# Eight expert slots behind the last gate, their order from the counts of 15 groups, and results written to (token, choice) rows

## The reference

```
conv   = grouped conv1d(x over the channels, 9 taps, 4 groups) + cond @ c_weight.T + bias
logits = conv @ W_gate + b_gate                    # 8 experts
i1, i2 = top_k(logits, 2)
x      = x + mean_k relu(conv @ W_e[i_k] + b_e[i_k])
att    = softmax(MLP(cond))                        # 8 weights per sample
x      = x + (sum_k att_k W_k applied to x over the channels + bias) @ dequant(qweight) + bias
```

## Time and profile before

| | us |
|---|---|
| median of 3 runs | 546.04 |
| lowest, highest | 544.32, 546.64 |
| the profiled execution, its time | 544.99 |
| the profiled execution, its span | 543.2 |
| PE busy | 513.6 |
| DVE busy | 339.4 |
| POOL busy | 147.0 |
| ACT busy | 121.7 |

### The profile page before, as it was taken

One profiled execution on the slowest core, in us unless ns is written; L12 is line 12 of the kernel. 1 busy time (PEld: TensorE's weight loads), 2 busy tenths in 40 slices (PEclk: granted clock), 3 DMA queues, 4 the chain that ended last, 5 costly groups with the idle time before them and its releaser, 6 DMA issues. The chain is left out here.

```text
span 543.2 us, 10445 instructions
## 1 busy us (share of the span) xinstructions
PE 513.6 (95%) x2486; PEld 344.6 (63%) x2487; DVE 339.4 (62%) x1003; ACT 121.7 (22%) x277; POOL 147.0 (27%) x162
## 2 busy tenths in 40 slices
PE   6969999999978999999999999999979899999996
PEld 5859999999955344444444444444427677777774
DVE  3466888888873563333333333333762899999996
ACT  2122223234310111111111111111121222222221
POOL 8042444544463000000000000000004766556520
PEclk9999999999988999999999999999998999999999
DMA  4999778877444844444444444444465899888862
GB/s 116 379 319 330 254 242 298 289 272 239 170 154 149 213 155 151 155 155 155 155 155 154 153 151 154 151 151 157 128 218 174 266 312 294 291 276 288 299 199 97
DMA packets 84823, 114.32 MB, mean 210 GB/s; under 512 B 15197, under 2 KB 51853, under 8 KB 83509
## 3 DMA queue, kind: packets, MB, share of 16 engines
q1 hardware_dynamic: 57936, 56.49, 32.5%
q0 software_dynamic: 10528, 33.75, 18.8%
q10 hardware_dynamic: 16328, 23.72, 12.5%
HBM read 67.48 MB, written 46.45 MB: 210 GB/s over the span
## 5 line engine op out<-in xcount | busy, mean ns | idle before, releaser
L989 PE MATMUL bank<-we,hT 128*128 x536 | 230.9, 593 | 4.0 <-DVE hT L815 4.0
L989 PEld LDWEIGHTS bank<-we,hT 128*128 128x128 f32 x536 | 101.5, 190 | 132.3 <-issue 132.1
L454 POOL DMA_INDIRECT we<-result_d,gidx x64 | 68.4, 1069 | 284.9 <-issue 276.9
L824 DVE TENSOR_TENSOR ring_a<-bank,be_bc 128x512 f32<-128x512 f32 x71 | 48.9, 689 | 126.4 <-PE bank L989 117.9
L957 PE MATMUL bank<-wconv,phases 128*128 128x128 f32 x768 | 93.0, 279 | 4.9 <-ACT phases L478 4.9
L957 PEld LDWEIGHTS bank<-wconv,phases 128*128 128x128 f32 x768 | 90.2, 195 | 5.3 <-ACT phases L478 5.3
L532 ACT ACTIVATE ring_b<-ring_a 128x512 f32<-128x512 f32 x71 | 44.7, 630 | 208.2 <-DVE ring_a L824 201.6
L435 POOL DMA_INDIRECT lists_d<-htok,row_i x64 | 62.9, 983 | 87.6 <-issue 63.4
L815 DVE STREAM_TRANSPOSE hT<-htok 128x512 f32<-128x512 f32 x71 | 49.8, 701 | 9.0 <-DMA htok<-lists_d 9.0
L1029 PE MATMUL bank<-mix_bd,we 128*128 128x128 f32 x256 | 36.6, 286 | 2.3 <-DVE we L858 2.3
L945 PE MATMUL bank<-wg,hT 128*128 128x136 f32 x256 | 37.4, 289 | 1.1 <-ACT htok L488 1.1
(11 more groups left out here) (164 smaller groups left out, 406.4 us busy)
## 6 DMA issues: line engine op xcount, KB each, us to landing
htok<-lists_d SPq DMA_DIRECT2D x284, 64.0 KB, 2.4
result_d<-ring_b ACTq DMA_DIRECT2D x71, 256.0 KB, 2.4
xt<-in_x SPq DMA_DIRECT2D x64, 256.0 KB, 4.3
we<-in_L_ffn_W_e SPq DMA_DIRECT2D x8, 1024.0 KB, 6.5
out<-orow SPq DMA_DIRECT2D x32, 256.0 KB, 3.9
lists_d<-orow SPq DMA_DIRECT2D x8, 256.0 KB, 7.5
be_bc<-in_L_ffn_b_e ACTq DMA_DIRECT2D x1, 2048.0 KB, 11.2
rows_r<-ctx_d SPq DMA_DIRECT2D x1, 1920.0 KB, 10.7
```

What stands on the lines that cost most here:

```text
L454: pool.indirect_dma_start(found[:, j, k, :], None, result_d, bass.IndirectOffsetOnAxis(ap=gidx[:, j, k:k + 1], axis=0), bounds_check=NT * ...
L824: dve.tensor_tensor(ring_a[:, j % 2, :], ps_exp[j % 2][:, :], be_bc[:, bass.ds(expert, 1), :].rearrange("p a n -> p (a n)"), ALU.add).then ...
L989: mm = pe.matmul(ps_exp[j % 2][:, :], hT[:, j % 2, p * P:(p + 1) * P], we[:, bass.ds(expert, 1), p, :].rearrange("m a n -> m (a n)"), star ...
```

## The change

It has four parts.

1. **Early slots.** `base` after 15 groups is turned into a first table, `tab_early`, by 19 small DVE operations spread over groups 16 to 26 (`early_table`). It names 8 slots, all of them full blocks of 128 rows that those 15 groups have already filled. SP loads the first four behind the scatters of the 15 groups. PE runs slot 0 directly behind the last gate, and the rank counts, the mixing kernels and the table's transpose between slots. The 34 idle transposes are gone. The final table counts the taken blocks out, and its slots follow from slot 8 on; the number of products stays the same.
2. **(token, choice) rows.** Each row of a list gets two more numbers (`LK` = 514): 2 x token, and the first choice's expert. A row is now 2,056 bytes. ACT writes them (L532 of the new kernel), SP loads them with a fifth DMA per slot (`keys`, 8 bytes a row), and DVE makes the pair's row from them (`pair_i`). A pad row has a key beyond the bound and is skipped.
3. **Result stores.** POOL scatters a slot's results by one indirect DMA to `pairs_d`, in place of ACT's direct store. Stage 3 loads the two results of a group by one direct DMA of 512 KB from SP, in place of POOL's two gathers; `find_places` and the index copies on ACT are gone.
4. **Order and buffers.** Lists load into `xt`, four slots ahead, and DVE transposes two slots ahead into four buffers (`lT`, of which `hT` is two). Side work moves: mixing bias to slot 6, masks and dequantizing to slots 9 to 13, the rank rows to 17 to 19. Loops over groups are looped up to group 16 instead of 24.

The core of the diff:

```diff
+            for s in range(NT):
+                pool.wait_ge(result_ready, s + 1)
+                pool.wait_ge(pair_ready, s + 1)
...
+                pool.indirect_dma_start(pairs_d, bass.IndirectOffsetOnAxis(ap=pair_i[:, s % DR:s % DR + 1], axis=0),
+                                        ring_b[:, s % U, :], None, bounds_check=2 * N * C - 1,
+                                        oob_is_err=False).then_inc(result_out[s % U], 16)
...
-            sp.wait_ge(head_out, 16 * E)
-            for s in scattered:
-                sp.wait_ge(s, 32 * (NG // U))
-            sp.wait_ge(tab_ready, 2)
+            sp.wait_ge(early, N_EARLY)
+            for j, s in enumerate(scattered):
+                sp.wait_ge(s, 32 * len(range(j, counted, U)))
...
+                    if isinstance(a, int) and a == EARLY:
+                        sp.wait_ge(head_out, 16 * E)
+                        for i, scat in enumerate(scattered):
+                            sp.wait_ge(scat, 32 * len(range(i, NG, U)))
+                        sp.wait_ge(tab_ready, 2)
...
+                    sp.dma_start(keys[:, ja, :], lists_d[bass.ds(row, P), L:LK]).then_inc(list_in[ja], 16)
...
+            def load_pairs(a):
+                sp.dma_start(found[:, a % FR, :, :], pairs_g[a]).then_inc(pairs_in[a % FR], 16)
+
+            for i, s in enumerate(result_out):
+                sp.wait_ge(s, 16 * len(range(i, NT, U)))
+            for g in range(U):
+                load_pairs(g)
...
+            def transpose_list(a, ja):
+
+                wait(dve, list_in[ja], (a - ja) * (80 // XR) + 80)
+                wait(dve, exp_done, a - AHEAD + 1)
+                dve.transpose(lT[:, ja, :].rearrange("m (p h r) -> m h p r", p=PH, h=MH),
+                              xt[:, ja, :].rearrange("r (h p l) -> r h p l", h=MH, p=PH)).then_inc(lT_ready, 1)
+                wait(dve, result_out[ja], 16 * ((a - DR - ja) // U + 1))
+                dve.scalar_tensor_tensor(pair_i[:, a % DR:a % DR + 1], keys[:, ja, 1:2], slot_expert[:, a:a + 1],
+                                         keys[:, ja, 0:1], ALU.not_equal, ALU.add).then_inc(pair_ready, 1)
...
+            for g in range(hi1, NG - 2):
+                step1_late(g, g % U)
+            early_wait()
+            transpose_list(0, 0)
+            step1(NG - 2, (NG - 2) % U)
+            transpose_list(1, 1)
+            step1(NG - 1, (NG - 1) % U)
+            dve.wait_ge(tok_done, NG - 1)
+            transpose_list(2, 2)
+            step1(NG, NG % U)
+            dve.wait_ge(tok_done, NG)
+            transpose_list(3, 3)
+            dve.wait_ge(be_in, 16)
+            add_bias(0, 0)
+            step1(NG + 1, (NG + 1) % U)
+            add_bias(1, 1)
...
-            for _ in range(WARM):
-                pe.transpose(bank[6][:, 0:P], ident[:, :], ident[:, :])
...
+            gate_and_rows(NG - 1, (NG - 1) % U)
+            pe.wait_ge(early, N_EARLY)
+            pe.wait_ge(we_in, 16 * E)
+            product(0, 0)
+            count_ranks(NG - 2, (NG - 2) % U)
+            product(1, 1)
+            count_ranks(NG - 1, (NG - 1) % U)
+            mix_layers(NG + 1 - mlp_first)
+            for s in range(2, 5):
+                product(s, s % U)
+            pe.wait_ge(tab_ready, 1)
+            pe.transpose(ps_misc[0:3, 256:256 + P], tab_f[:, :], ident[:, :]).then_inc(tab_done, 1)
+            pe.matmul(ps_misc[:, 256 + P:256 + 2 * P], tab_f[:, 1:2].to_broadcast((P, P)), ident[:, :], start=True, stop=True).then_inc(tab_done, 1)
+            for s in range(5, EARLY):
+                product(s, s % U)
+            pe.wait_ge(tab_ready, 2)
+            stepped(pe, step2, lo2, 16, hi2, NT)
```

More of the change, by code:

```diff
@@ L32 @@
 XR = 4
+FR = 8
+DR = 8
+LK = L + 2
+NO_PAIR = 1 << 20
+EARLY = 8
+AHEAD = 4
 RS = B + 2
@@ L265, in build_program @@
         table = sem("table")
+        early = sem("early")
         tab_done = sem("tab_done")
@@ new lines, in load_x @@
+            def load_x(a):
+                sp.dma_start(htok[:, a % XR, :], x_g[a]).then_inc(x3_in[a % XR], 16)
+            for s in range(-U, lo2):
+                list_step(s, s % U)
+            for g in range(XR):
+                load_x(g)
+            stepped(sp, list_step, lo2, lo2, hi2 - U, NT - U)
+            def load_pairs(a):
+                sp.dma_start(found[:, a % FR, :, :], pairs_g[a]).then_inc(pairs_in[a % FR], 16)
+            for i, s in enumerate(result_out):
+                sp.wait_ge(s, 16 * len(range(i, NT, U)))
@@ L479, in step1 @@
                              ps_ph[:, :].rearrange("k (h s l) -> k h s l", h=MH, s=SUB)).then_inc(ph_ready, 1)
+                b = g - 2
+                if live(b, NG):
+                    jb = (j - 2) % U
+                    wait(act, expert_ready, b + 1)
+                    act.copy(token_list[:, jb, L:LK],
+                             expert_of[:, bass.ds(b, 1), 0:2].rearrange("p a k -> p (a k)")).then_inc(key_ready, 1)
                 a = g - 1
@@ L544, in _, with store_mix @@
-            for s in range(SUB):
-                rows = slice(s * C, (s + 1) * C)
-                act.dma_start(mix_bd[rows, :, rows],
-                              mix_d.rearrange("(g s) i o -> s i g o", s=SUB)[s]).then_inc(mix_in, 16)
-            stepped(act, step2, 1, lo2, hi2, NT)
+            def store_mix():
+                act.wait_ge(mlp_ev, 11)
+                act.wait_ge(mixb_split, 3)
+                act.dma_start(mixb_d[0], mixb_hi[:, :].bitcast(F32)).then_inc(mix_out, 16)
+                act.dma_start(mixb_d[1], mixb_lo[:, :].bitcast(F32)).then_inc(mix_out, 16)
+                act.dma_start(mix_d, mix_sb[:, :, :]).then_inc(mix_out, 16)
@@ new lines, in load_mix @@
+            def load_mix():
+                act.wait_ge(mixbd_zero, 1)
+                act.wait_ge(mix_out, 48)
+                act.wait_ge(mixb_one, 1)
+                for half in range(2):
+                    pair = 2 * B + 2 * half
+                    act.dma_start(token_rows[pair:pair + 2, :].bitcast(F32),
+                                  mixb_d[half:half + 1].rearrange("a n c -> a (n c)").to_broadcast((2, N * C))).then_inc(mix_in, 16)
+                for s in range(SUB):
+                    rows = slice(s * C, (s + 1) * C)
+                    act.dma_start(mix_bd[rows, :, rows],
+                                  mix_d.rearrange("(g s) i o -> s i g o", s=SUB)[s]).then_inc(mix_in, 16)
@@ L550, in step3 @@
+            for s in range(lo2):
+                step2(s, s % U)
+                if s == 6:
+                    store_mix()
+            for s in range(lo2, 12):
+                step2(s, s % U)
+                if s == 8:
+                    load_mix()
+            stepped(act, step2, 12, 12, hi2, NT)
             def step3(g, j):
@@ new lines, in add_bias @@
+            def add_bias(s, j):
+                if isinstance(s, int) and s < EARLY:
+                    expert = dve.value_load(tab_early[0:1, 1, s:s + 1], min_val=0, max_val=E - 1)
+                else:
+                    expert = dve.value_load(tab[1:2, bass.ds(s - EARLY, 1)], min_val=0, max_val=E - 1)
+                wait(dve, exp_done, s + 1)
+                wait(dve, result_ready, s - 1)
+                dve.tensor_tensor(ring_a[:, j % 2, :], ps_exp[j % 2][:, :],
+                                  be_bc[:, bass.ds(expert, 1), :].rearrange("p a n -> p (a n)"), ALU.add).then_inc(sum_ready, 1)
@@ L790, in find_places @@
-            def find_places(first, last):
-                rows2 = row_of[:, :, :].rearrange("p g k -> p (g k)")
-                expert2 = expert_of[:, :, :].rearrange("p g k -> p (g k)")
-                for e in range(first, last):
-                    if e == 0:
-                        then(dve.tensor_scalar(shift_s[:, :], expert2, 0.0, offs[:, 0:1], ALU.is_equal, ALU.mult))
-                    else:
-                        then(dve.tensor_scalar(shift_e[:, :], expert2, float(e), offs[:, e:e + 1], ALU.is_equal, ALU.mult))
-                        then(dve.tensor_tensor(shift_s[:, :], shift_s[:, :], shift_e[:, :], ALU.add))
-                if last == E:
-                    dve.tensor_tensor(place_i[:, :, :].rearrange("p g k -> p (g k)"), rows2, shift_s[:, :], ALU.subtract).then_inc(place_ready, 1)
```

310 lines of the change are left out of this document (178 added, 132 removed).

## The result

The changed kernel takes **538.56 us**, median of 4 runs (536.77 to 540.77); the kernel before, measured beside it, takes 545.96 (4 runs, 544.32 to 546.64). The ratio is 0.9868, with a 95% interval of [0.9838, 0.9897]: faster by 7.4 us. Forecast were 530.0 and a range of 526 to 538. The direction was right, the gain less than half of the 15.6 us that the sum gave, and the time lies just above the range. A second set of runs, beside its own runs of the kernel before, gives 0.9857 (experiment 9).

A forecast was written before the change was run, and what follows sets the result against it. PE was taken to bound all three stages. Takeover -13.2, handover -1.0 and start of stage 3 -1.4 sum to -15.6, from the profiled 544.99 to 529.4; half of 1.05 put back gives 530.0 us, range 526 to 538.

The forecast's parts named there:

- Does one wait?: Check of the takeover into stage 2: no early product waits, and product 8 has a slack of 4 to 5 us.
- Stage 2, 0: Steady expert slots: no change in time, queue work fits each 3.43 us slot, fifth load covered by four slots of lead.
- bound of -9: Smallest gain allowed for the takeover into stage 2, if one product waits a full slot's time; the other bound was -15.
- the -13.2 forecast: Takeover from last gate into stage 2: 16.1 us of gap and stalls can go, 2.9 stay on PE.
- Handover, -1.0: From last product to stage 3's first mixing: about 1.0 us gained through sooner idle matmuls and direct loads, range -3 to +4.
- The second rival: Longer handover to stage 3: 512 KB loads land after 8.6 us, not 3.4, giving 535 us; chance 8%.
- The rule of the Trainium skill that I weighed: Handover: issue DMAs under DVE's work from ACT or SP, not GpSimd; by it the sum would be 2.8 us higher.
- Start of stage 3, -1.4: From first to third mixing in stage 3: 6.52 us becomes 5.1 with groups 0 to 3 loaded in one go.
- Stage 1, 0 (to +2): Stage 1: added table operations and longer scatter rows cost PE nothing, range 0 to +2 us.
- The takeover stalls: Rival at the start of stage 2: a list, table or bias is late once, giving 535 us; chance 10%.
- The 72% for 530: Whole kernel: the chance given to the time coming out as forecast, 530.0 us.
- the signs named ahead: Traces of being right: product 0 within 0.5 us of last gate, clock 1.00, mixing kernels 1.8 us, last product near 390.5.

The follow-up runs named there:

- experiment 9: The changed kernel, unaltered, run and profiled a second time: 537.53 us, ratio 0.9857.
- experiment 3: Changed kernel with stage 3's x loads issued behind the last list and the mixing load behind slot 24, not 8: 531.71 us, ratio 0.9748.
- experiment 7: experiment 3 with both last rank counts and the mixing kernels put back ahead of product 0: 538.41 us, ratio 0.9866.
- experiment 5: experiment 3 without each list's fifth load (keys), result rows made from slot number and lane: 531.72 us, ratio 0.9739.
- experiment 10: experiment 3 with the quantized words' eight loads spread over groups 16 to 23 and the biases' load at 24, not group 3: 527.38 us, ratio 0.9639.
- experiment 12: experiment 3 with only the 2 MB load of the biases moved, to group 24: 529.14 us, ratio 0.9614.
- experiment 8: The kernel before, unchanged, profiled a second time: 542.78 us, one run.
- experiment 11: The kernel before with the words' eight loads at groups 24 to 31 and the biases' load at 31, not group 3: 547.99 us, ratio 0.9956.
- experiment 1: Changed kernel with only the four x loads for stage 3 moved, behind the last list: 533.05 us, ratio 0.9769.
- experiment 2: Changed kernel with only the mixing load moved, from behind slot 8 to behind slot 24: 532.94 us, ratio 0.9755.
- experiment 6: experiment 5 with list rows of 2,048 bytes again, not 2,056: 531.59 us, ratio 0.9744.

## Why the prediction was right or wrong

**Where it failed: "Does one wait?" and "Stage 2, 0", both terms that the x loads and the mixing load should have been in.** I followed product by product up to slot 8, found slacks of 4 to 5 us, and stopped where the table was in use. For the rest I wrote "four slots of lead are 13.7 us" and took the queues' work per slot, 1.6 us of 3.43 on SP, as if each slot had the same. The diff puts four loads of 256 KB into SP's queue between lists 11 and 12 and the mixing load behind slot 8 on ACT. Neither has a term in my sum, though the 1.36 us in the earlier trace rows stand right behind such a load at its old place. Measured, the two together cost 7.3 us, 4.94 of waiting and most of the rest low clock (6.1 in the second profile). My bound of -9 for the term allowed one late product and no fall of the clock; the profile showed -5.3.

**The term's mechanism and size were right where nothing meets.** In experiment 3, gate end to last product end is 234.7 us against 247.3, so -12.6 against the -13.2 forecast. The idle time of the kernel before, its low clock and its waits in the first slots did go, and experiment 7 shows that the order of counts and products carries 6.7 us of it.

**Handover, -1.0.** In experiment 3: 15.09 us against 16.12, so -1.0. In the changed kernel +0.1: the idle matmuls took 12.69 us and not 11.25, and ended at 417.5, after the data. This isn't a cost of the stall: the changed kernel's second profile has the stall, 11.27 us of idle matmuls and 15.10 us of handover, and experiments 5, 10 and 12 have no stall and 15.8 to 15.9. The three profiles of the kernel before and its variant have 15.84 to 16.21. So the -1.0 was met in about half of the profiles; the sum took the length of the idle matmuls as fixed, and it changes with the clock by 1 us and more. The data path had the forecast's length: the last result scatter is issued at 408.74, 7.6 us after the last product's end (forecast 7.0), the first pairs' load at 410.94, and DVE's first addition starts at 414.80:

```profile
414.80 0.69 DVE L987 TENSOR_TENSOR we<-token_list,we 128x512 f32<-128x512 f32 x1 [8.60 <-DMA we<-pairs_d]
```

That is T + 13.65; my steps put it at 10.3 + 3.4 = 13.7. The second rival, loads that land after 8.6 us, didn't come: DVE starts 3.86 us after the issue begins, and the median of all 32 is 4.7.

**POOL as issuer beside DVE.** The page's group says what the result scatters cost:

```profile
L506 POOL DMA_INDIRECT pairs_d<-ring_b,pair_i x71 | 70.5, 992 | 164.7 <-DVE pair_i L867 112.1
```

71 issues at a mean of 992 ns, against 980 in the earlier trace rows, so POOL's issues weren't longer beside DVE's work. The rule of the Trainium skill that I weighed, in "SBUF — State Buffer", section "Summary: rules for kernel authors", speaks of DVE in its 2x and 4x perf modes alone. I had taken it for all of DVE's work, and no run here shows whether an operation of DVE was in such a mode.

**Start of stage 3, -1.4:** -1.9, a little small; 4.58 to 4.71 us in all eleven profiles with the change, 6.52 to 6.70 in three without it. **Stage 1, 0 (to +2):** PE's pace is unchanged, but its beginning is not; two traces against nine give about +2 at convolution 7, from a cause that stays open (experiments 8 to 12). I had looked at 60 to 80 us alone, where the stage is steady.

**The rivals.** "The takeover stalls", 10% at 535, was what happened, with the price too small: it took one product's time and no clock loss. It was named for a list, the table or a bias within the sequence that I had followed, not for the loads that came behind it. The 72% for 530 was too much for a sequence that I had followed through 8 slots of 71. Of the signs named ahead, product 0's distance, the mixing kernels and the steady convolutions came out as written; the full clock throughout and the absence of idle time did not, and the last product ended at 401.2 where 390.5 was named. The sign of being wrong, idle time ahead of products 5 to 8, didn't show either: the wait came at product 12.

## What to carry to other kernels

When a change removes a gap, list every DMA that it puts into the stretch behind it, on all queues, with bytes and packet size, and follow the loads until the lead is full again, not only until the handover is done. Two loads that are each harmless there may not be together; move one of them to where the lead is full (here 6 to 7 us for a few moved lines). And count a PE wait of some microseconds dearer than its length: here 4.94 and 3.49 us in stage 2 were followed by about 2.1 and 1.7 us lost to the low clock, though not every wait of that length was (below).

## What the runs showed of the hardware that was not expected

- Four loads of 128 KB in pieces of about 142 bytes occupied ACT for 7.33 us beside the x loads, for 4.05 us in experiment 1 without them, and for 3.77 us in experiment 3. ACT's next operation, the relu at 202.72, stood idle 7.69 us behind it.
- With the engines' share at 1.26, a list of four 64 KB loads and the keys was there 7.4 us after its last issue and 9.7 after its first; in experiment 2, without the mixing load, 2.8 and 4.9 us after them.
- Behind PE's idle time of 4.94, 3.49 and 2.44 us the granted clock fell to 0.50. In the kernel before once more, 3.47 us of idle time ahead of convolution 5 left it at 1.00, and so did 3.7 us ahead of experiment 6's idle matmuls. In experiment 10 it fell to 0.56 at 162 to 166 us, where PE had been busy since 152.46 behind idle times of 1.05 and 0.75 us. So the length of the last idle time alone doesn't decide it.
- Loading the lists from rows of 2,056 bytes took 1.23 times the DMA engines' time that it took from rows of 2,048 (experiments 5 and 6, 28,519 and 28,573 packets), scattering the rows 1.04 to 1.07 times.
- The same program reaches convolution 7 up to 2.2 us earlier or later from one execution to the next; from there to convolution 31 its profiles agree within 0.03 us.
